# Products of the identity matrix with itself, added to five waits of TensorE in a chain of Sinkhorn scaling, gated feed-forward, GRU, attention and routed experts

## What is computed

```python
# x: (B=128, N=32, D=128)
K = exp(-x / 0.1); K = K / K.sum((-2, -1))
for _ in range(31):                       # Sinkhorn scaling, stopped when u moves under 1e-9
    v = c / (K^T u); u = r / (K v)
P = u * K * v^T                           # transport plan, (B, N, D)
x1 = x + ffn0(P)                          # sigmoid router, 8 experts (two of them weighted in) and a shared one, relu squared
y  = gru(x1, h0=cond)                     # 32 steps in order; after each fourth step h = tanh(h Wp + bp)
y  = y + attention(layernorm(y))          # 16 heads of 8, over the 32 positions
y  = y + experts1(layernorm(y))           # the best of 8 experts for each token, gelu, 128 -> 512 -> 128
```

## Time and profile before

| | us |
|---|---|
| median of three runs | 531.68 |
| the profiled execution | 531.67 |
| its span, first to last instruction | 529.9 |
| TensorE busy / weight loads | 471.5 / 386.6 |
| VectorE, ScalarE, GpSimd busy | 356.7, 328.0, 238.6 |
| mean granted TensorE clock | 0.961 |

### The profile page before, as it was taken

One profiled execution on the slowest core, in us unless ns is written; L12 is line 12 of the kernel. 1 busy time (PEld: TensorE's weight loads), 2 busy tenths in 40 slices (PEclk: granted clock), 3 DMA queues, 4 the chain that ended last, 5 costly groups with the idle time before them and its releaser, 6 DMA issues. The chain is left out here.

```text
span 529.9 us, 23933 instructions
## 1 busy us (share of the span) xinstructions
PE 471.5 (89%) x8960; PEld 386.6 (73%) x8960; DVE 356.7 (67%) x1278; ACT 328.0 (62%) x822; POOL 238.6 (45%) x587
## 2 busy tenths in 40 slices
PE   0799999999959998999999985799999978989992
PEld 0589999999956644666666673588888868979992
DVE  4778788887867584666657654367999985734440
ACT  4545555555535864556566566368878877967770
POOL 3134444444445000054433445734577755775552
PEclk9999999999989999999999998589999997999997
DMA  8253000000000056242222000800011116265200
GB/s 242 82 175 108 0 0 0 0 0 0 0 1 0 3 135 133 60 81 80 80 85 80 1 1 1 315 6 2 11 53 43 54 57 184 97 177 143 64 33 10
DMA packets 24192, 34.39 MB, mean 65 GB/s; under 512 B 3616, under 2 KB 17957, under 8 KB 23752
## 3 DMA queue, kind: packets, MB, share of 16 engines
q1 hardware_dynamic: 21360, 27.23, 17.9%
q0 software_dynamic: 2784, 6.56, 3.4%
HBM read 25.98 MB, written 8.26 MB: 65 GB/s over the span
## 5 line engine op out<-in xcount | busy, mean ns | idle before, releaser
L217 ACT ACTIVATE den_v<-ps_g,floor 128x128 f32<-128x128 f32 x124 | 45.5, 368 | 46.1 <-PE ps_g L241 42.2
L255 PE MATMUL ps_g<-buf_b,v_pad 128*32 128x128 f32 x1984 | 67.3, 276 | 2.3 <-DVE v_pad L335 1.4
L241 PE MATMUL ps_g<-buf_a,u_pad 128*32 128x128 f32 x1984 | 68.1, 278 | 0.3
L241 PEld LDWEIGHTS ps_g<-buf_a,u_pad 128*32 128x32 f32 x1984 | 53.9, 112 | 2.1 <-DVE u_pad L350 1.1
L255 PEld LDWEIGHTS ps_g<-buf_b,v_pad 128*32 128x32 f32 x1984 | 50.8, 110 | 3.2 <-DVE v_pad L335 1.9
L728 PE MATMUL ps_h<-buf_c,up 128*128 128x512 f32 x96 | 50.0, 617 | 0.3
L1382 POOL DMA_INDIRECT out<-buf_d,token_i x39 | 38.8, 995 | 24.9 <-DVE buf_c L1898 18.3
L335 DVE RECIPROCAL v_pad<-ps_g 128x32 f32<-128x32 f32 x124 | 39.0, 334 | 14.1 <-PE ps_g L247 11.8
L199 POOL TENSOR_SCALAR held_u<-inv_u 128x8 f32<-128x8 f32 x124 | 24.6, 198 | 45.7 <-DVE inv_u L344 44.9
L1389 POOL TENSOR_TENSOR vb<-vn,row_mask 128x1024 f32<-128x1024 f32 x16 | 30.3, 1892 | 29.9 <-PE ps_o L1498 20.4
L1595 PE MATMUL ps_ss<-xT,buf_d 128*128 128x128 f32 x312 | 43.2, 283 | 0.2 <-issue 0.2
(11 more groups left out here) (368 smaller groups left out, 1229.4 us busy)
## 6 DMA issues: line engine op xcount, KB each, us to landing
cw_b<-cw_d SPq DMA_DIRECT2D x16, 512.0 KB, 7.8
buf_c<-sorted_x SPq DMA_DIRECT2D x39, 136.0 KB, 2.2
buf_a<-in_x SPq DMA_DIRECT2D x4, 512.0 KB, 6.5
buf_b<-in_x_t SPq DMA_DIRECT2D x4, 512.0 KB, 7.2
buf_d<-in_x_nt SPq DMA_DIRECT2D x1, 2048.0 KB, 10.2
x<-in_w SPq DMA_DIRECT2D x1, 2048.0 KB, 7.7
buf_b<-in_w SPq DMA_DIRECT2D x1, 2048.0 KB, 13.3
sorted_x<-nobody SPq DMA_DIRECT2D x1, 1088.0 KB, 10.3
```

Source lines behind the costliest of these rows:

```text
L217: fn(den_v[:, h, :], ps_v[h], ACT.Relu, bias=floor[:]).then_inc(v_den, 1)
L241: last = mm(ps_v[h][32 * j:32 * j + 32, :], u_pad[:, h, j, 32 * i:32 * i + 32], K[:, t * D:(t + 1) * D], start=i == 0, stop=i == TI - 1)
L255: last = mm(ps_u[h][32 * c:32 * c + 32, :], v_pad[:, h, c, 32 * i:32 * i + 32], KT[:, b * N:(b + BG) * N], start=i == 0, stop=i == TI - 1)
```

## The change

TensorE gets 45 further products, each of the 128 x 128 identity with itself, float32, into a part of PSUM whose former content has been read. Nobody reads them and they raise no semaphore. They stand at these places of TensorE's stream:

- 6 behind the last Sinkhorn round, with a wait for the last round's `u_ready[0]` before them;
- 9 behind the one product of the short block;
- 4 behind the last GRU step, before `turn_step(31)`, with a wait for `r_out` of 5 before them (the copy that frees the bank they write), 14 between `turn_back` of pairs 12, 13 and that of pairs 14, 15, and 5 behind the last `turn_back`;
- 7 behind the two register reads and before the first `turn_rows` of the experts.

```diff
@@ sinkhorn, block.tensor
                     one_round(i, False)
                     one_round(i + NG, False)
+                pe.wait_ge(u_ready[0], NG * (ITERS + 1))
+                for _ in range(6):
+                    mm(ps_g[0][:, 0:P], ident[:], ident[:], start=True, stop=True)
@@ the short block
                 nc.tensor.matmul(ps_s[0:1, 0:ITERS], ones[:, 0:1], moved[:, :, 0], start=True, stop=True).then_inc(s["overs"], 1)
+                for _ in range(9):
+                    nc.tensor.matmul(ps_g[0][:, 0:P], ident[:], ident[:], start=True, stop=True)
@@ plan_ffn_gru, block.tensor
+                def stay_warm(count):
+                    for _ in range(count):
+                        mm(ps_h[0][:, 0:P], ident[:], ident[:], start=True, stop=True)
+
+                pe.wait_ge(r_out, 5)
                 pe.wait_ge(st.out, TAIL // 2 - 2)
+                stay_warm(4)
                 turn_step(N - 1)
-                for pair in range(TAIL // 2 - 2, N // 2):
-                    turn_back(pair)
+                turn_back(TAIL // 2 - 2)
+                turn_back(TAIL // 2 - 1)
+                stay_warm(14)
+                turn_back(TAIL // 2)
+                turn_back(N // 2 - 1)
+                stay_warm(5)
@@ attend_route_experts, block.tensor
                          for n in range(EARLY_TABLE // PACK)]
+                for _ in range(7):
+                    mm(ps_h[0][:, 0:P], ident[:], ident[:], start=True, stop=True)
                 turn_rows(0)
```

## The result

| | runs | median us | lowest to highest |
|---|---|---|---|
| before | 14 | 530.80 | 527.96 to 533.84 |
| after | 14 | 528.45 | 525.95 to 530.44 |

The ratio is 0.9952, with a 95% interval of 0.993 to 0.9975: by this ratio 2.5 us less, between 1.3 and 3.7 (the two medians differ by 2.35). The forecast was 6.2 us less. The profiled execution of the changed kernel took 528.58 us, with a span of 526.8 us and a mean granted clock of 0.987 (before: 531.67, 529.9 and 0.961).

The account below looks back on a forecast made before the run. TensorE, busy nine tenths of nearly every slice, was taken as the bound where its clock halved after idling, with other engines waiting. Gains 0.9 + 3.4 + 1.9 = 6.2 us took 531.67 to 525.5 us; range 523.4 to 529.3.

Parts of the forecast that it names:

- A: End of Sinkhorn, 6 and 9 products: hidden in waits, they keep the clock up; gain 0.9 us, bounds 0 and 2.
- B: End of the GRU into attention, 4, 14 and 5 products: gain 2.6 + 0.8 = 3.4 us, bounds 2.3 and 4.8.
- C: Start of the experts, 7 products before the first `turn_rows`: gain 1.9 us, bounds 0 and 2.4.
- Rival 3: Products don't hold the clock and get in the way at all places: 3.8 us slower, 535.4 us; chance 0.06.
- Rival 1: Clock survives the wait before attention's body 1 too: 7.5 us gained, 524.2 us; chance 0.22.
- rival 2: Less won: C brings nothing or B keeps only 2.6 us; 3.5 us gained, 528.2 us; chance 0.16.
- So I expect it to stay up: At A: gaps left of 0.8, 1.0 and 0.3 us are each below the 1.36 us the clock survived.
- The block's end was to cost nothing: At B: the last five products end later than VectorE and give back the 0.3 us won before them.
- Gain 1.9 us: At C: 4.84 us of dense work at half clock, half to win, less a wait for ScalarE; first `join` about 2.1 us earlier.
- The profiled execution is as good as the median of the runs: Base of the sum: profiled 531.67 us against a median of 531.68, so nothing was added.
- The rule weighed: Skill's rule that the clock falls after gaps above about 3 us; doubted, since 2.28 us idle went with a fall.

Follow-up runs that it names:

- b_closed: Kernel before plus only the 4, 14 and 5 products at B and ten more before attention's body 1; 525.94 us, 0.9923 of before.
- holes_no_c: Changed kernel plus four products in A's open gap and ten before attention's body 1, without the seven at C; 542.94 us, 0.9929 of before.
- a_closed: Kernel before plus only the 6 and 9 products at A and four more in the gap left there; 545.28 us, 0.998 of before.
- c_only: Kernel before plus only the seven products at C; 546.16 us, 0.9987 of before.
- a_only: Kernel before plus only the 6 and 9 products at A; 544.79 us, 0.9979 of before.
- b_only: Kernel before plus only the 4, 14 and 5 products at B; 544.01 us, 0.9966 of before.
- set 4: Follow-up runs of b_closed, after_fourth and the changed kernel with A's and B's gaps filled, on a chip like the first; before took 530.24 us.
- no_five: Changed kernel without the five products behind the last `turn_back`; 546.99 us, 0.9974 of before.
- after_fourth: The changed kernel, unaltered, run again in set 4; 527.23 us, 0.9946 of before.
- set 1: Follow-up runs of each place's products alone and of the changed kernel again, on another chip; before took 546.66 us.
- set 2: Follow-up runs that filled open gaps, added products at Sinkhorn's start or left out the last five at B; before took 548.30 us.

## Why the prediction was right in sign and wrong in size

**The mechanism held, with exceptions.** The clock stayed up at A in all five traces and at B in all six in which every gap was filled. Where a gap was left, it fell at B each time and at A in five of eight; at C it fell just ahead of the products, or as they began, in two of eleven. The forecast was 3.7 us too high. By the terms as all traces together give them (below), A's is 0.9 too high, C's 0.9 and B's 1.5. Rival 3 is refuted: a batch of 28 records took 3.29 us and one of 8 took 1.06, so 20 more records cost 2.23, that is 0.22 us a product as priced, plus about 0.17 us for a batch. Rival 1 (warm throughout) is out as well: around the wait before body 1 the clock fell in all seven traces that have B's products and that gap open. Of the cases named, less won (rival 2, 3.5 us) is the nearest to the 2.5 us measured, but not quite by its route: B kept 2.7 us in the profiled pair, as it said, and A's 0.9 were missing; at C the clock stayed up in that pair, and the products delayed the first transpose by 0.6 us.

**Which step failed at A: "So I expect it to stay up", and with it the 0.9 us.** The gaps were held one by one against the 1.36 us that the clock had survived. That was no safe bound even in the trace of before: at C its clock fell at 437.71, when TensorE had stood idle since 436.39, 1.32 us and not the 2.28 that the gap had in the end. And the last of the gaps was not seen: the step counted 0.8, 1.0 and 0.3 us up to the transposes, and did not ask what TensorE does when its transposes end 0.9 us earlier while VectorE's tile stays where it is. That is the 1.07 us gap. In eight traces with A's products and the gap open it stayed up in three (49.43 to 49.45 us) and fell in five (50.91 to 51.13); with the gap filled it stayed up in five of five. A late fall is worse than an early one, as it lies wholly in dense records: 0.6 to 0.8 us more than in the trace of before. But late falls come without A's products too, as `b_closed` shows: its 51.24 us and the 50.16 to 50.48 of the three others make 50.56 on average. Even where A's gain is won, some of it is waited away at the GRU's first step, which needs a DMA. VectorE's row in `holes_no_c`:

```profile
204.81 0.29 DVE L1088 TENSOR_TENSOR rh<-gate,h_in 128x128 f32<-128x128 f32 x1 [1.57 <-DMA cw_d<-buf_a]
```

This wait is 1.58 us on average in the seven traces in which the clock stayed up at A (`a_closed` with its slow stretch left out) and 1.20 in the four without A's products. From the first GRU product to the last step the seven took 122.17 us, the four 121.82: about 0.35 us given back, though single traces overlap. So A brings some 0.7 us when the clock stays up, costs 0.5 when it falls late, and with the gap left open brings nothing on average (50.44 us in eight traces against 50.56).

**At B the steps were right and the base was wrong.** `scores` of body 1 was forecast 2.55 us earlier and came 2.2 us earlier in the trace; the second fall came where it was forecast. The block's end was to cost nothing and costs 0.15 us. The gain to body 2 was 2.7 us in the profiled pair, for a term of 3.4: behind body 1 it was 0.5 for 0.8. What was mis-sized most is what the term is set against. One execution of before was priced, and in it the clock stayed down for 20.48 us. Of the four traces without B's products, before and c_only reached body 2 in 25.20 us, a_only and a_closed in 23.28 and 23.23. If both happen equally often, B is worth about 1.9 us, which is what the ratio of `b_only` gives as well (1.9 us, between 0.7 and 3.0); how often each happens isn't settled by four traces.

**At C the "Gain 1.9 us" was 0.8 in the pair.** The slow stretch was removed, as said, but half of its 4.8 us was not what the `join` waited for. The loads of the first tiles end last (1.40 us of waiting for `sorted_x` above), and the products themselves hold the first transpose by 0.4 to 0.6 us, and by some 2 where they ran at half clock. On this chip and the like one of set 4 the interval took 7.8 us with the seven products (8.48, 7.32, 7.66) and 8.8 without (9.29, 8.26): 1.0 us, from five traces that spread by 1 us. On the other chips it took 8.9 us with them (mean of eight) and 8.8 without (mean of four): nothing.

**The sum and its base.** About 0 + 1.9 + 1.0 us comes to 2.9; measured are 2.5 us, between 1.3 and 3.7. "The profiled execution is as good as the median of the runs" was true of three runs, all within 1.2 us; fourteen spread over 5.9 us with a median of 530.80, and the profiled one had the long stretch at B.

**The rule weighed.** The Trainium skill, "TensorE: Matmul & The Clock Gate", section "Why this matters for your kernels", puts the limit at gaps of about 3 us. These runs disagree: it fell with waits of 1.9 to 2.3 us before body 1 each time, and in some executions with single gaps no longer than 1.07 us (A) or 1.20 us (no_five).

## What to carry to other kernels

Work that nobody reads can hold TensorE's clock, at 0.22 us for a float32 product of 128 x 128, but in these traces only filling every gap around the dense work did so each time: when a wait is filled, look at the gaps that the faster work opens behind it, and fill those too; and let the products start before the clock falls: at C they come behind a wait of 1.0 us, and in two of eleven traces they started too late. Price a slow stretch by what another engine waits for in it, not by its length, and read more than one execution before doing so, as the moment of the fall differs between runs of the same kernel. A block's last products may cost a little (0.15 us here) and still pay, if the gap behind them is the one over which the clock would fall.

## What the runs showed of the hardware that was not expected

The same gaps, equal to 0.01 us, bring the clock down in one execution and not in the next; waits of 1.9 to 2.3 us before body 1 did so in all nine traces in which the clock was up ahead of them, the series of 0.8, 0.3 and 1.1 us in five of eight.

Time at half clock was cheap. Taking it for each run as (1 − mean clock) x 2 x time, the 17 runs of before in set 4 had 37.1 us of it and the 12 of after_fourth 12.0: 25 us fewer at half clock, for 3.0 us less time. Over the runs of before in the four sets it went with the time at 0.09 to 0.26 us for each us at half clock (correlation 0.80 over the 35 runs of set 1, but 0.34 over the 17 of set 2). That much of this time lies beside waits for other engines and for DMAs is shown at C, and for the rest it is argued.
